# One loop instead of three in a gated feed-forward stage, with the norm and the down projection inside the tile loop

## The reference, cut to what matters

```python
xn = layernorm(x)
# branch 1: a Mamba2 mixer, then a gated feed-forward layer, both with residuals
h  = xn + mamba2_mixer(rmsnorm(xn, norm_w), ...)
u  = rmsnorm(h, post_norm_w)
a  = h + (silu(u @ gate_w.T) * (u @ up_w.T)) @ down_w.T      # 1024 -> 2752 -> 1024
# branch 2: a second gated layer with weights given as integers, scaled by 1/127
f  = (silu(xn @ wg.T) * (xn @ wu.T)) @ wd.T                  # 1024 -> 3072 -> 1024
return x + a + f
```

## Time and profile before

| what | us |
|---|---|
| time, median of 2 runs (4528.77 to 4529.22) | 4528.99 |
| the profiled execution's own time | 4532.43 |
| its span on the slowest core (core 0) | 4530.9 |
| spans of the eight cores | 4504.3 to 4530.9 |
| TensorE, busy in the span | 2263.3 |
| DVE, busy | 1830.2 |
| ACT, busy | 520.5 |

### The profile page before, as it was taken

The page is one execution under the profiler, slowest core; times in us unless marked ns, Lnnn a source line. Parts: engine busy times, 40 slices in busy tenths (PEclk is TensorE's granted clock), DMA queues, the critical chain, the costliest instruction groups (busy, mean ns, idle before and its releaser), DMA issues.

```text
span 4530.9 us, 36531 instructions; the slowest of 8 cores (4504.3 to 4530.9 us)
## 1 busy us (share of the span) xinstructions
PE 2263.3 (50%) x9681; PEld 1008.3 (22%) x9681; DVE 1830.2 (40%) x3927; ACT 520.5 (11%) x981; POOL 103.9 (2%) x152
## 2 busy tenths in 40 slices
PE   0526503438850333333434331677765806878877
PEld 0212201113320111111111110333332302333333
DVE  3532595653129565656575753122220101222222
ACT  3000020000122221212121211000000000000000
POOL 0110000000000000000000000000000000000000
PEclk9998855559975555555555555888887958988988
DMA  5552000011120310111011116100006582111111
GB/s 162 190 156 59 19 0 1 1 40 22 53 60 0 84 66 33 66 33 66 33 66 38 61 48 131 36 26 20 20 29 143 150 158 44 49 33 33 49 33 35
DMA packets 136658, 265.56 MB, mean 59 GB/s; under 512 B 69680, under 2 KB 70480, under 8 KB 135824
## 3 DMA queue, kind: packets, MB, share of 16 engines
q0 software_dynamic: 35200, 117.97, 11.0%
q1 hardware_dynamic: 98960, 136.86, 10.0%
q10 hardware_dynamic: 2304, 8.39, 0.5%
HBM read 255.06 MB, written 63.19 MB: 70 GB/s over the span
## 4 chain that ended last, share of the span: by engine, by line
PE 42%; DVE 21%; issue 16%; DMA 11%; another core or an unknown queue 4%; ACT 4%; DVEq 1%; SPq 0%; ACTq 0%; POOL 0%; POOLq 0%
PE P L1049 4%; PE P L1226 4%; PE P L1230 4%; PE P L1053 3%; PE P L926 3%; PE P L1119 3%; PE P L420 3%; PE P L425 3%; DMA wbuf<-w_in 3%; DVE Emt L842 3%; DMA bcast<-lam_dram 2%; PE P L1265 2%; PE PS L1265 2%; PE P L645 2%
## 5 line engine op out<-in xcount | busy, mean ns | idle before, releaser
L848 PE MATMUL P<-x_tok,Emt 128*128 128x64 bf16 x512 | 108.3, 212 | 284.7 <-DVE Emt L842 275.6
L549 DVE SCALAR_TENSOR_TENSOR B_acc<-xbc,c_convw,B_acc 128x2048 bf16<-128x2048 bf16 x108 | 245.4, 2346 | 0.0
L1247 DVE TENSOR_TENSOR F_h<-F_h,P 128x1024 bf16<-128x1024 bf16 x48 | 58.6, 1222 | 441.5 <-ACT F_h L1241 441.5
L1226 PE MATMUL P<-wg,F_xf 128*128 128x512 bf16 x384 | 146.2, 381 | 170.7 <-DMA wd2b<-w_d 125.5
L1069 DVE TENSOR_TENSOR E_h<-E_sg,P 128x1024 bf16<-128x1024 bf16 (+1 forms) x48 | 53.3, 1110 | 425.6 <-ACT E_sg L1065 425.6
L1049 PE MATMUL P<-wg,hnT 128*128 128x512 bf16 x384 | 160.5, 442 | 112.4 <-DMA wu<-w_u 70.3
L833 ACT ACTIVATE Est<-Est 128x128 f32<-128x128 f32 x512 | 154.7, 308 | 424.3 <-DVE Est L827 422.9
L1119 PE MATMUL P<-wd,E_h2t 128*128 128x512 bf16 x704 | 163.2, 391 | 79.5 <-DMA wd<-w_d 52.6
L332 PE MATMUL P<-c_identf,A_n 128*128 128x128 f32 x256 | 90.6, 445 | 198.0 <-DVE A_n L320 166.3
L842 DVE SCALAR_TENSOR_TENSOR Emt<-Est,dtk,Gm 128x128 bf16<-128x128 f32 x512 | 175.6, 345 | 8.4 <-PE P L848 5.2
L1241 ACT ACTIVATE F_h<-P 128x1024 bf16<-128x1024 f32 x48 | 49.2, 1024 | 1070.7 <-PE P L1230 1070.7
(11 more groups left out here) (197 smaller groups left out, 4070.0 us busy)
## 6 DMA issues: line engine op xcount, KB each, us to landing
bcast<-lam_dram SPq DMA_DIRECT2D x64, 512.0 KB
A_x<-x_own SPq DMA_DIRECT2D x32, 512.0 KB, 4.2
A_x<-x_pre SPq DMA_DIRECT2D x32, 512.0 KB, 4.3
E_h<-h_dram SPq DMA_DIRECT2D x32, 512.0 KB, 3.4
h2t_dram<-E_h2t POOLq DMA_DIRECT2D x16, 704.0 KB, 4.8
E_h2t<-h2t_dram SPq DMA_DIRECT2D x16, 704.0 KB, 6.8
wd<-w_d POOLq DMA_DIRECT2D x2, 5376.0 KB, 77.5
xn_dram<-A_n POOLq DMA_DIRECT2D x16, 512.0 KB, 4.9
```

What stands on the lines that cost most here:

```text
L549: e.scalar_tensor_tensor(a[:, :], xbc[:, ec * CW + k:ec * CW + k + T], self.c["convw"][:, ec * 4 + k:ec * 4 + k + 1], a[:, :], ALU.mult, A ...
L1226: e.matmul(slots[j][:, 0:512], xft[p][:, dc * 128:(dc + 1) * 128], w[:, dc * INTER2 + cb:dc * INTER2 + cb + 512], start=(dc == 0), stop=(d ...
```

## The change

Phase E becomes one loop over tiles, with the down projection in it, and its three weights are loaded together at the start.

- `wd1` gets a place of its own behind `wu1`. The buffers for activations move to the region where `hnT` was. `hnT` becomes two buffers of one tile.
- The four weight loads are issued by POOL at the start of the phase, and PE waits for the last before any of its work in the phase.
- The norm of a tile is a function `front(i)`. It is called for tile 0 ahead of the loop, and for tile i+1 after the gate and up parts of tile i and ahead of the 22 transposes of tile i. So in ACT's queue Square, Ln and Exp of tile i+1 stand behind the third Silu of tile i and ahead of the first Silu of tile i+1. In PE's queue 8 transposes of tile i+1 stand ahead of the 22 of tile i.
- Silu writes into `h2` and the product is made in place there.
- The 44 down matmuls of a tile follow its transposes at once, into `P1` and `PS`, and wait for the last transpose's copy. The addition is split in two. The path through `h2t_dram` is gone, and so is the second load of `h1t`: the load of tile i+1 waits for the store of tile i-1.

```diff
+        ldd = self.op("gpsimd", ... wd1 <- w_d1, 21 blocks of rows)
+        lddb = self.op("gpsimd", ... wd1 <- w_d1, last 64 rows)
+        self.wait("tensor", "dw", lddb)
...
+        def front(i):
+            p = i % 2
+            dhp = "dh%d" % p
+            t_ldh[i] = self.op("sync", lambda e, i=i, p=p: e.dma_start(
+                h1t[p][:, :], self.h1_dram[ts(i), :]),
+                wait=[("dn%d" % p, t_sp.get(i - 2))], inc=(dhp, 16))
+            a1 = self.op("scalar", ... AF.Square, accum_out=ssqE[:, p:p + 1]),
+            a2 = self.op("scalar", ... AF.Ln ...
+            t_rms[i] = a3 = self.op("scalar", ... AF.Exp, scale=-0.5),
+            t_vh[i] = self.op("vector", lambda e, p=p: e.scalar_tensor_tensor(
+                hn[p][:, :], h1t[p][:, :], ssqE[:, p:p + 1], c["postw"][:, :],
+                ALU.mult, ALU.mult),
+            for dc in range(NDC):
+                t_hnt[i] = transpose(dc, hn[p][:, ts(dc)], hnTt[p][:, ts(dc)], ...
...
+        front(0)
         for i in range(NTIL):
...
+            if i + 1 < NTIL:
+                front(i + 1)
             t_tr = None
             for k in range(22):
...
-            t_sp[("sp", i)] = self.op("gpsimd", lambda e, i=i, p=p: e.dma_start(
-                bass.AP(self.h2t_dram.tensor, i * 128,
-                        [[22 * T, 128], [T, 22], [1, 128]]), h2t[p][:, :]),
-                wait=[("sv", t_tr)], inc=("dn%d" % p, 16))
-        self.barrier()
...
-        for i in range(NTIL):
...
-            ldt = self.op("sync", lambda e, i=i, p=p: e.dma_start(
-                h2t[p][:, :], bass.AP(self.h2t_dram.tensor, i * 128, ...
+                for q, pb in ((0, P1), (1, PS)):
+                    mm = self.op("tensor", lambda e, k=k, q=q, pb=pb, kp=kp: e.matmul(
+                        pb[:, 0:512], h2t[0:kp, k * 128:(k + 1) * 128],
+                        wd1[0:kp, k * DM + q * 512:k * DM + (q + 1) * 512],
+                        start=(k == 0), stop=(k == 21)),
+                        wait=([("sv", t_tr), ("sv", t_v1b.get(i - 1))]
+                              if k == 0 and q == 0 else []),
```

More of the change, by code:

```diff
@@ L949, in phase_E @@
     def phase_E(self):
-        import os as _os
         cv = self.carve
         c = self.c
-        P0, P1, PT = self.P0, self.P1, self.PT
-        hnT = cv("hnT", OFF["R_B"], [128, NDC * T], BF16)
+        P0, P1, PT, PS = self.P0, self.P1, self.PT, self.PS
         wg1 = cv("wg1", OFF["R_C"], [128, NDC * INTER1], BF16)
         wu1 = cv("wu1", OFF["R_D"], [128, NDC * INTER1], BF16)
-        EST = OFF["R_D"] + 45088
-        h1t = [cv(f"E_h1{p}", EST + p * 4096, [128, DM], F32) for p in range(2)]
@@ L959, in phase_E @@
[L959 to L962, removed]
-               for p in range(2)]
[L964 to L985, removed]
@@ L987, in phase_E @@
-        t_ld = {}
-        t_rms = {}
-        t_vh = {}
-        for i in range(NTIL):
[L991 to L1017, removed]
@@ L1018, in phase_E @@
-        t_hnT = self.cnt["sv"]
+        wd1 = cv("wd1", OFF["R_D"] + 44032, [128, 22 * DM], BF16)
+        h1t = [cv(f"E_h1{p}", OFF["R_B"] + p * 4096, [128, DM], F32)
+               for p in range(2)]
+        hn = [cv(f"E_hn{p}", OFF["R_B"] + 8192 + p * 2048, [128, DM], BF16)
+              for p in range(2)]
+        hnTt = [cv(f"E_hnT{p}", OFF["R_B"] + 12288 + p * 2048, [128, NDC * 128],
+                   BF16) for p in range(2)]
+        h2 = cv("E_h2", OFF["R_B"] + 16384, [128, INTER1], BF16)
@@ L1020, in phase_E @@
+        h2t = cv("E_h2t", OFF["R_B"] + 21888, [128, 22 * 128], BF16)
+        sqscr = cv("E_sqs", OFF["dt2"], [128, DM], F32)
+        ssqE = cv("E_ssq", OFF["devscr"], [128, 2], F32)
         ldg = self.op("gpsimd", lambda e: e.dma_start(
@@ L1027, in phase_E @@
             inc=("dw", 16))
-        self.wait("tensor", "dw", ldu)
+        ldd = self.op("gpsimd", lambda e: e.dma_start(
+            bass.AP(wd1, 0, [[22 * DM, 128], [DM, 21], [1, DM]]),
+            bass.AP(self.w_d1.tensor, 0, [[DM, 128], [128 * DM, 21], [1, DM]])),
+            inc=("dw", 16))
+        lddb = self.op("gpsimd", lambda e: e.dma_start(
+            bass.AP(wd1, 21 * DM, [[22 * DM, 64], [1, DM]]),
+            bass.AP(self.w_d1.tensor, 21 * 128 * DM, [[DM, 64], [1, DM]])),
+            inc=("dw", 16))
@@ new lines, in phase_E, with transpose @@
+        self.wait("tensor", "dw", lddb)
+        slotA_b = P1[:, 640:704].bitcast(BF16)
+        slotB_b = PT[:, 256:384]
+        t_slot = {0: None, 1: None}
+        def transpose(idx, src_ap, dst_ap, xtra_tr=(), xtra_ev=()):
+            q = idx % 2
+            pp = slotA_b if q == 0 else slotB_b
+            np_ = src_ap.shape[0]
+            nf = src_ap.shape[1]
+            tt = self.op("tensor", lambda e, pp=pp, s=src_ap, np_=np_, nf=nf:
+                         e.transpose(pp[0:nf, 0:np_], s, c["ident"][0:np_, 0:np_]),
+                         wait=[("sv", t_slot[q])] + list(xtra_tr), inc=("st", 1))
+            t_slot[q] = self.op("vector",
+                                lambda e, pp=pp, d=dst_ap, nf=nf, np_=np_:
+                                e.tensor_copy(d, pp[0:nf, 0:np_]),
+                                wait=[("st", tt)] + list(xtra_ev), inc=("sv", 1))
+            return t_slot[q]
@@ new lines, in phase_E @@
+        t_ldh = {}
+        t_rms = {}
+        t_vh = {}
+        t_hnt = {}
+        t_ttl = {}
+        t_guT = {}
+        t_h2tt = {}
+        t_v1b = {}
+        t_sp = {}
+        def front(i):
[4 more added lines that the diff above has]
+                wait=[("dn%d" % p, t_sp.get(i - 2))], inc=(dhp, 16))
+            a1 = self.op("scalar", lambda e, p=p: e.activation(
+                sqscr[:, :], h1t[p][:, :], AF.Square, accum_out=ssqE[:, p:p + 1]),
+                wait=[(dhp, t_ldh[i]), ("sa", t_rms.get(i - 1))], inc=("sa", 1))
+            a2 = self.op("scalar", lambda e, p=p: e.activation(
+                ssqE[:, p:p + 1], ssqE[:, p:p + 1], AF.Ln, bias=EPS_RMS,
+                scale=1.0 / DM), wait=[("sa", a1)], inc=("sa", 1))
+            t_rms[i] = a3 = self.op("scalar", lambda e, p=p: e.activation(
+                ssqE[:, p:p + 1], ssqE[:, p:p + 1], AF.Exp, scale=-0.5),
+                wait=[("sa", a2)], inc=("sa", 1))
+            t_vh[i] = self.op("vector", lambda e, p=p: e.scalar_tensor_tensor(
+                hn[p][:, :], h1t[p][:, :], ssqE[:, p:p + 1], c["postw"][:, :],
+                ALU.mult, ALU.mult),
+                wait=[("sa", a3), ("st", t_ttl.get(i - 2))], inc=("sv", 1))
+            for dc in range(NDC):
+                t_hnt[i] = transpose(
+                    dc, hn[p][:, ts(dc)], hnTt[p][:, ts(dc)],
+                    xtra_tr=[("sv", t_vh[i])] if dc == 0 else (),
+                    xtra_ev=[("st", t_guT.get(i - 2))] if dc == 0 else ())
+            t_ttl[i] = self.cnt["st"]
@@ L1029, in phase_E @@
         parts = [(0, 1024), (1024, 1024), (2048, 704)]
         slots = [P0[:, 0:1024], P0[:, 1024:2048]]
-        t_sp = {}
-        t_sil = {}
         t_silu_u = {}
         t_spu = {}
+        t_dn = {}
         uu = 0
[L1036 to L1039, removed]
+        front(0)
@@ L1040, in phase_E @@
         for i in range(NTIL):
             p = i % 2
-            t_h2tr = None
+            dhp = "dh%d" % p
             for pi, (cb, cn) in enumerate(parts):
@@ L1078, in phase_E @@
                 t_tr = transpose(k, h2[:, k * 128:k * 128 + ncols],
[L1079 to L1082, removed]
-            t_sp[("sp", i)] = self.op("gpsimd", lambda e, i=i, p=p: e.dma_start(
-                bass.AP(self.h2t_dram.tensor, i * 128,
-                        [[22 * T, 128], [T, 22], [1, 128]]), h2t[p][:, :]),
-                wait=[("sv", t_tr)], inc=("dn%d" % p, 16))
-            self._t_h2 = self.cnt["sv"]
-        self.barrier()
[L1090 to L1106, removed]
-                h1t[p][:, :], self.h1_dram[ts(i), :]),
-                wait=[("sv", t_upd.get(i - 2)), ("dn%d" % p, t_st.get(i - 2))],
-                inc=(dhp, 16))
-            ldt = self.op("sync", lambda e, i=i, p=p: e.dma_start(
-                h2t[p][:, :], bass.AP(self.h2t_dram.tensor, i * 128,
-                                      [[22 * T, 128], [T, 22], [1, 128]])),
-                wait=[("sv", t_upd.get(i - 2)), ("dn%d" % p, t_sp.get(("sp", i)))],
-                inc=("de%d" % p, 16))
+                                 h2t[0:ncols, k * 128:(k + 1) * 128],
+                                 xtra_tr=[("sv", t_h2full)] if k == 0 else ())
+            t_h2tt[i] = self.cnt["st"]
             mm = None
@@ L1117, in phase_E @@
                 kp = 128 if k < 21 else 64
[L1118 to L1121 removed]
+                for q, pb in ((0, P1), (1, PS)):
+                    mm = self.op("tensor", lambda e, k=k, q=q, pb=pb, kp=kp: e.matmul(
+                        pb[:, 0:512], h2t[0:kp, k * 128:(k + 1) * 128],
                         wd1[0:kp, k * DM + q * 512:k * DM + (q + 1) * 512],
                         start=(k == 0), stop=(k == 21)),
```

(10 more changed lines are left out.)

43 lines of the change are left out of this document (17 added, 26 removed).

## The result

| | before | changed |
|---|---|---|
| median of all runs, us | 4528.99 (10 runs) | 4566.64 (12 runs) |
| ratio to before | | 1.0082, interval 1.0050 to 1.0113 |
| profiled execution, span of the slowest core | 4530.9 (core 0) | 4560.3 (core 1) |
| phase E, mean over the eight cores | 930.1 (925 to 936) | 957.1 (948 to 965) |
| the same on the slowest core | 935.7 | 961.4 |

Three of the 12 runs of the changed kernel and one of the 10 before were executions in which the cores of one die ran longer at a lower granted clock; the ratio leaves them out, and without them the medians are 4554.0 and 4528.8.

The account below looks back on a forecast made before the run. Weight loads were taken as bound by transfer, the loops by PE. Start 133.9, 15 periods 783 and tail 27.6 gave phase E 944.7 us against 935.7, + 9: 4538 us predicted, range 4514 to 4571.

Parts of the forecast that it names:

- Weights: Start of phase E: one load of three weights takes 103.1 us, third Silu of tile 0 at 133.9 us.
- From the third Silu to the first transpose: Each tile: Silu, a table load and the next tile's norm take 5.3 us, where it was 1.89.
- The rival of a long gap: ACT must run empty ahead of each table switch: + 10 us or more, 4548; chance 9%.
- the one of hidden tables: Table loads cost no time on the path, placed elsewhere or hidden: - 59 us, 4479; chance 5%.
- Transposes: Each tile: 30 transposes and the last copy ahead of the down matmuls take 11.2 us.
- Clock: PE's low clock per tile: 1.8 us at the down burst's head, 1.35 on average after the wait ahead of part 1.
- The upper end of the range: 4571 us, including 12 us for a longer low-clock loss at the start of the down burst.
- Four cases in five: Share of waits ahead of part 1 after which PE's clock falls, losing 1.69 us each time.
- Tail: From the third Silu of tile 15 to the end of phase E: 27.6 us with the split addition.
- That the clock doesn't fall in the waits: Rival: PE keeps its high clock after the 2.5 us waits: - 20 us, 4518; chance 17%.
- That it stays low through the burst: Rival: PE's clock stays low for a tile's whole down burst: + 120 us, 4658; chance 3%.
- The faster case: Faster by over 2%: needs 6.6 us less per tile, nearly all the norm's exposed 9.0; chance 2%.

Follow-up runs that it names:

- experiment 3: Changed kernel with Ln and Exp replaced by two multiply-adds on DVE, so no table loads (norm's scale wrong): ratio to before 0.9933, phase E 902.0 us.
- experiment 2: Changed kernel with the next tile's Square, Ln, Exp and scaling behind the first Silu instead of the third: ratio to before 0.9912, phase E 881.5 us.
- experiments 2 and 4: Number 4: changed kernel with all tiles' norm made ahead of the loop while weights load, h1 loaded again: ratio to before 0.9815, phase E 849.9 us.
- the late wait: PE waits for the down weights only ahead of the first down matmul; alone on the changed kernel: ratio to before 1.0037, phase E 941.0 us.
- the fastest one: Changed kernel with all norms under the weight load and down weights waited for late: median 4439.12 us, ratio to before 0.9772.
- experiment 1: Changed kernel, but PE waits for the down weights only ahead of the first down matmul: ratio to before 1.0037, phase E 941.0 us.
- experiment 7: Changed kernel with 22 useless matmuls on PE behind part 0's up product, filling the 2.7 us wait: ratio to before 1.0014, phase E 937.5 us.
- experiments 2, 8: Number 8: changed kernel with the next norm behind the first Silu and down weights waited for late: ratio to before 0.9797, phase E 853.9 us.

## Why the prediction was right, and where its sizes were off

The forecast was 4538 with a range of 4514 to 4571. The median is 4566.6, inside and near its upper end (4554.0 by the runs that the ratio uses). The side was right (no change of more than 2%), the size was not: + 9 us forecast for phase E, + 27 measured.

- **Weights.** 103.1 us were forecast, 104.7 passed on core 1 until PE's first work (2703.69 to 2808.41). The third Silu of tile 0 came at 134.7 us, forecast 133.9. The step held.
- **From the third Silu to the first transpose.** 5.3 forecast, 5.3 measured. One load of 1.28 us in each direction, with a gap of 0 or 0.35 us ahead of it. The rival of a long gap is out, and so is the one of hidden tables: without them 55 us went (experiment 3).
- **Transposes.** 11.2 forecast, 11.7 measured. In the timeline of phase F the first four of the 12 pairs ran at the high clock and took 0.70, and the forecast took that over. Here all 15 pairs run at the low one, in 0.74, two of them in 0.81 and 0.85, and from the last pair to the first down matmul it is 0.1 us longer: 0.5 x 15 = 8 us.
- **Clock.** This is the other term that was mis-sized. I took the loss at the head of the burst as fixed, 1.8 us, and the loss after the 2.7 us wait as an independent 1.35 (four cases in five). The runs show them together. In a long tile both occur, in a short one the second is absent and the first is small, 3.5 us apart. The forecast's stretches with the table load give 19.8 to the first Silu and 15.9 to the third; measured are 20.4 and 15.8 on core 1. So the first was 0.6 us too small, 9 us in all. The upper end of the range had 12 us for just this. The agreement of the second stretch is luck: a short tile takes 14.75 there and not 14.5, since PE waits 2.71 and 1.38 us where it waited 2.54 and 1.26, and the loss of clock was 1.03 and not 1.35.
- **Four cases in five.** The share came from one core. Over all eight cores of the kernel before, 9 of the 19 waits for loads of 1.97 to 3.39 us in the down loop were followed by 8 or 9 slow matmuls, and the 2.54 us wait of tile 0 on 5 cores, not on the 3 others. On core 1 it left the clock alone, against the earlier trace rows on core 0:

```profile
2848.54 0.38 PE L1049 MATMUL P<-wg,hnT 128*128 128x512 bf16 x1 [2.54 <-ACT E_sg L1065]
2848.76 0.38 PE L1053 MATMUL P<-wg,hnT 128*128 128x512 bf16 x1
2848.97 0.38 PE L1049 MATMUL P<-wg,hnT 128*128 128x512 bf16 x1
```

That is half of the cases, and half is what the changed kernel shows, 65 of 120. The share does not carry over to another order of the queues: in experiment 2 it was 8 of 120.

- **Tail.** 27.6 forecast, 28.7 measured.

The terms close on core 1: 134.7 + 15 x 53.2 + 28.7 = 961.4, the measured phase. Against the 944.7 of the sum (its terms as printed add up to 944.5) it is 15 us of period and 2 of the ends. That makes 25.7 us from slowest core to slowest core, and 27.0 on the mean of the cores.

- **The rivals.** That the clock doesn't fall in the waits: true of 5 to 9 of 15 tiles, not of the kernel. That it stays low through the burst: no, 14 slow matmuls at most. The faster case had no room in the changed order, as said. With another order of the same queues it was there (experiments 2 and 4), and order, the place of the norm and the late wait together are what separates the changed kernel from the fastest one, 957.1 and 835.5 us of phase E.

What stays open is what sets a tile long or short. An edit ahead of the loop changes the share (experiment 1), and PE's standing still is needed for the second loss (experiment 7), but the same 2.7 us wait ahead of part 2 cost the clock in 0 to 2 of 15 tiles (experiments 2, 8). No run separates the length of what came before from its place in time.

## What to carry to other kernels

Fusing a stage saves its round trip and its barrier, but each piece of the stage now stands somewhere in an engine's queue. Put the next tile's serial chain where that engine is idle anyway (behind the first Silu and not the third, here 76 us), and work of another function table in a stage of its own or under a load. A loss of clock of a few matmuls can come and go with an edit ahead of the loop, so compare the cut-up tile and not the total before you credit an edit with a gain or a loss. And take the share of such a loss from all the cores of the profile: one core gave four in five, all eight gave half.

## What the runs showed of the hardware

- A table load stood behind the wait of its own ACTIVATE each time and was not made ahead, though ACT was idle: 16 of 16 loads at L1068 followed the wait for PE, 597.2 us of idle time in all. The drain of about 1380 ns that the Trainium skill gives in "ScalarE: Activation LUTs", section "What ACT_TABLE_LOAD costs", is not in this trace: the 15 loads at L1020 have 1.4 us of idle time ahead of them in all, and the ACTIVATE behind the load at 2894.56 starts 0.02 us after its end.
- 22 matmuls without use, 1.39 us a tile, made the phase 19.6 us shorter.
- The granted clock fell up to two matmuls after a wait had ended, at 0.49 and 0.63 us behind a first one of 0.38, and the same wait in the same loop left it alone in other tiles. The slow matmuls at the head of the burst and those after the wait came together in 65 of 120 tiles of the changed kernel, and there never the second without 13 or 14 of the first.
